# First attention in batches of four cells: one cell per row group, six score banks in three rotating pairs

## The reference, cut to what matters

```python
q = _l2norm(proj(Wq)); k = _l2norm(proj(Wk)); v = proj(Wv)
attn = jnp.einsum('bhqd,bhkd->bhqk', q, k)
rel = pos[None, :] - pos[:, None]
mask = (rel < 0) | (rel >= WINDOW)
bias = jnp.where(mask[None], NEG_INF, -abs(rel) * slopes[:, None, None])
attn = jax.nn.softmax(attn + bias[None], axis=-1)
out = jnp.einsum('bhqk,bhkd->bhqd', attn, v)     # then @ Wo.T, and x = x + out
```

## Time and profile before

| | us |
|---|---|
| median of 3 runs | 460.81 |
| lowest, highest | 457.39, 463.28 |
| profiled execution | 462.66 |
| its span (first to last instruction) | 460.9 |
| PE busy | 380.2 (83%) |
| DVE busy | 261.1 (57%) |
| ACT busy | 163.3 (35%) |
| POOL busy | 141.0 (31%) |

### The profile page before, as it was taken

How to read it: one execution, slowest core, us unless ns; L and a number is a source line. 1 busy time by engine, 2 the same in 40 slices (tenths; PEclk the granted TensorE clock), 3 DMA queues, 4 the chain that set the end, 5 groups by cost and what they waited for, 6 DMA issues and landing times.

```text
span 460.9 us, 12653 instructions
## 1 busy us (share of the span) xinstructions
PE 380.2 (83%) x5430; PEld 285.8 (62%) x5430; DVE 261.1 (57%) x708; ACT 163.3 (35%) x294; POOL 141.0 (31%) x191
## 2 busy tenths in 40 slices
PE   2889999887976706999913679999988998899997
PEld 1677888776856704777711336766765786566665
DVE  7336868876876001444429268776766689633332
ACT  1345547354541303333313222433332304333331
POOL 4012533441428772444425201112112200222221
PEclk9797899999995556999985578999998998899999
DMA  8970200006004112111130000000000000000000
GB/s 239 182 196 1 83 4 4 3 6 253 4 3 146 34 54 72 48 55 47 32 108 0 1 0 4 1 3 3 1 4 4 3 0 2 0 2 23 23 24 23
DMA packets 16199, 19.54 MB, mean 42 GB/s; under 512 B 1376, under 2 KB 14432, under 8 KB 15568
## 3 DMA queue, kind: packets, MB, share of 16 engines
q1 hardware_dynamic: 14896, 16.17, 13.1%
q0 software_dynamic: 1248, 2.57, 1.8%
HBM read 13.60 MB, written 5.13 MB: 41 GB/s over the span
## 4 chain that ended last, share of the span: by engine, by line
PE 64%; DVE 17%; POOL 6%; issue 5%; ACT 3%; DMA 3%; POOLq 0%; SPq 0%; DVEq 0%
PE ps L396 6%; PE ps L1228 4%; PE ps L1310 4%; PE ps L1197 4%; PE ps L374 4%; PE ps L795 3%; POOL xs L1001 3%; PE ps L778 3%; PE ps L779 3%; PE ps L1212 3%; DVE RP L517 3%; PE ps L1237 3%; PE ps L1289 3%; PE ps L1294 2%; PE ps L317 2%
## 5 line engine op out<-in xcount | busy, mean ns | idle before, releaser
L517 DVE TENSOR_TENSOR RP<-ps,RC 128x1440 f32<-128x1440 f32 (+2 forms) x30 | 46.5, 1573 | 8.0 <-PE ps L374 7.9
L659 ACT ACTIVATE RP<-RP 128x1440 f32<-128x1440 f32 (+2 forms) x30 | 40.2, 1340 | 30.1 <-DVE RP L517 30.1
L1562 POOL TENSOR_TENSOR RA<-RA,sm 128x512 f32<-128x512 f32 x18 | 18.8, 1047 | 89.5 <-DVE sm L1404 89.5
L1568 POOL TENSOR_TENSOR RP<-RP 128x512 f32<-128x512 f32 x16 | 16.7, 1042 | 73.4 <-DVE RP L1435 73.4
L396 PE MATMUL ps<-RP,RA 128*32 128x160 f32 (+4 forms) x736 | 33.1, 259 | 4.4 <-DVE LGS L542 3.1
L396 PE MATMUL ps<-RP,con 128*32 128x160 f32 (+4 forms) x736 | 33.0, 256 | 2.7 <-issue 2.7
L691 POOL TENSOR_SCALAR RA<-sm,con 128x512 f32<-128x512 f32 x13 | 20.4, 1587 | 43.4 <-DVE sm L462 43.4
L1009 POOL DMA_INDIRECT ys<-RP x23 | 22.0, 958 | 37.1 <-ACT RP L973 28.1
L374 PE MATMUL ps<-RC,RA 32*128 32x160 f32 x512 | 31.2, 320 | 0.9 <-DVE RA L470 0.6
L884 DVE TENSOR_TENSOR RP<-RP,ps 128x352 f32<-128x352 f32 x23 | 12.0, 521 | 30.5 <-ACT RP L967 30.5
L374 PEld LDWEIGHTS ps<-RC,RA 32*128 32x128 f32 x512 | 25.3, 191 | 5.1 <-issue 2.9
(11 more groups left out here) (245 smaller groups left out, 864.9 us busy)
## 6 DMA issues: line engine op xcount, KB each, us to landing
RA<-in_gu SPq DMA_DIRECT2D x1, 2816.0 KB, 10.2
RB<-in_dw SPq DMA_DIRECT2D x1, 1536.0 KB, 21.2
xs<-zero SPq DMA_DIRECT2D x1, 1483.5 KB, 15.9
RP<-xs SPq DMA_DIRECT2D x5, 258.0 KB, 2.7
RC<-in_tz SPq DMA_DIRECT2D x1, 1120.0 KB, 5.6
X<-in_x SPq DMA_DIRECT2D x4, 256.0 KB, 5.0
XN<-ys SPq DMA_DIRECT2D x4, 256.0 KB, 3.6
out<-X SPq DMA_DIRECT2D x3, 256.0 KB, 2.3
```

Of the source, the lines that this page charges most:

```text
L517: e.tensor_tensor(out.rearrange("p k (i c) -> p k i c", i=n), bank.rearrange("p k (i c) -> p k i c", i=n), bias.unsqueeze(2).to_broadcast( ...
L659: e.activation(v, v, ACT.Exp).then_inc(S["exp"], 1)
L1562: e.tensor_tensor(heads32(m.AT[c % 4]), heads32(m.D1[c % 4]), over(m.R1_[c % 4], 32), ALU.mult).then_inc(S["at1"], 1)
```

## The change

Scores are made per batch: 12 products (24 records), strip by strip, each strip on the four row groups into four banks. Banks 0 to 5 are three *pairs*. A user takes a pair: the first and second half of a batch's scores (`h` = 0, 1: groups 0, 1 and 2, 3), the two halves of a serve, and an output (one pair). A user waits for the one three pairs back. PE's `scores(b)` waits for both of its pairs before its first product.

- VectorE adds the bias in two halves of 128 x 960, ScalarE takes exp in two halves. `P` is a ring of three batches.
- `pv(s)` is now called per strip, for batch b - 2 after the scores of batch b, and counts strips. Only the accumulations use banks 6 and 7; outputs go to a pair of the rotating banks, so the wait of `pv` for `finished` goes away.
- Output k is issued after the value products of batch `ends_in(k) + 2`, that is in loop `ends_in(k) + 4`: in loops 7, 10, 13, 15, 18, 21, 23, 23. Eviction and division of block k stand in loop `ends_in(k) + 2`: 5, 8, 11, 13, 16, 19, 21; ScalarE evicts between its two exps.
- The division's multiplication of blocks 0 to 6 moves from VectorE to GpSimd (`divided`), between the parts of `wide`, `keys` and `norm`. Block 7's stays on VectorE.
- Serves come after the scores of batches 0, 5 and 9. All four value copies of a serve are ScalarE's. A serve's first half is free again when `normal` has read it, its second when ScalarE has copied it.
- X gets rows of 136 words, 128 of X and 8 of logits, so `finished` is one addition of 272 elements.
- SyncE loads `gu` after 15 batches.

The diff, cut:

```diff
+SERVED = {0: 1, 5: 2, 9: 3}
+def last_strip(k):
+    return min(8 * k + 11, NSTRIP - 1)
+def ends_in(k):
+    return last_strip(k) // 3
+def outputs_after(b):
+    return [k for k in range(8) if min(ends_in(k) + 2, NB - 1) == b]
+def order_of_turns():
+    turns = []
+    for b in range(NB + 2):
+        if b < NB:
+            turns.append(("scores", b))
+        if b in SERVED:
+            turns.append(("serve", SERVED[b]))
+        if b >= 2:
+            turns += [("output", k) for k in outputs_after(b - 2)]
+    return turns
+TURNS = order_of_turns()
+PAIRS = [(kind, k, h) for kind, k in TURNS for h in range(1 if kind == "output" else 2)]
+def pair_of(kind, k, h=0):
+    return 2 * (PAIRS.index((kind, k, h)) % 3)
+def wait_pair(w, kind, k, h=0):
+    n = PAIRS.index((kind, k, h)) - 3
     if n >= 0:
-        kind, k = TURNS[n]
-        if kind == "set":
-            w.wait_ge("ad", k + 1)
+        kind, k, h = PAIRS[n]
+        if kind == "scores":
+            w.wait_ge("ad", 2 * k + h + 1)
+        elif kind == "output":
+            w.wait_ge("x1", k + 1)
+        elif h == 0:
+            w.wait_ge("qn", 2 * k + 2)
         else:
-            w.wait_ge("qn", 2 * k + 2)
-            w.wait_ge("vba", 2 * k + 2)
-            w.wait_ge("vbv", 2 * k + 2)
+            values_made(w, k)
...
     def serve(b):
-        wait_turn(w, "serve", b)
+        wait_pair(w, "serve", b, 0)
         expand(b)
+        wait_pair(w, "serve", b, 1)
         values(b)
...
+    def scores(b):
...
+        for h in range(2):
+            wait_pair(w, "scores", b, h)
+        for i in range(len(strips_of(b))):
...
+            for g in range(4):
+                r = slice(32 * g, 32 * g + 32)
+                t = e.matmul(PS[pair_of("scores", b, g // 2) + g % 2][:, 160 * i:160 * i + 160], m.KB[r, s, :, :],
+                             m.QT[r, 32 * s:32 * s + 160], start=True, stop=True)
         t.then_inc(S["sc"], 1)
...
+    def pv(s):
+        q, end = max(0, 32 * (s - 4)), 32 * (s + 1)
+        w.wait_ge("exp", 2 * (s // 3) + 2)
...
-                if k >= 3:
-                    w.wait_ge("x1", 2 * (k - 2))
...
+    for b in range(NB + 2):
+        if b < NB:
+            scores(b)
+        if b in SERVED:
+            serve(SERVED[b])
+        if b >= 2:
+            for s in strips_of(b - 2):
+                pv(s)
+            for k in outputs_after(b - 2):
                 output(k)
...
+    def biased(b, h):
+        n = len(strips_of(b))
+        w.wait_ge("sc", b + 1)
...
         w.wait_ge("dn", 3 * k + 2)
+        if k:
+            w.wait_ge("otn", k)
         e.transpose(m.RT, m.RS.rearrange("p (j h) -> p j h", h=4).unsqueeze(3).to_broadcast([128, 8, 4, 8])
                     ).then_inc(S["dn"], 1)
-        w.wait_ge("dn", 3 * k + 3)
-        if k >= 2:
-            w.wait_ge("mwo", k - 1)
-        e.tensor_tensor(m.OTN[k % 2], ev[:, 0:256], m.RT, ALU.mult).then_inc(S["otn"], 1)
+        if k == 7:
+            divided(e, w, S, m, 7)
...
+    for kind, b in TURNS:
+        if kind == "scores":
+            biased(b, 0)
+            biased(b, 1)
+            for k in range(7):
+                if ends_in(k) + 2 == b:
                     normed(k)
+        elif kind == "serve":
+            normal(b)
+        else:
+            if b == 7:
+                normed(7)
+            finished(b)
+            stats(b)
+def divided(e, w, S, m, k):
+    w.wait_ge("dn", 3 * k + 3)
+    if k >= 2:
+        w.wait_ge("mwo", k - 1)
+    e.tensor_tensor(m.OTN[k % 2], m.EV[k % 2][:, 0:256], m.RT, ALU.mult).then_inc(S["otn"], 1)
...
+    for kind, b in TURNS:
+        if kind == "scores":
+            weights(b, 0)
+            for k in range(7):
+                if ends_in(k) + 2 == b:
                     out(k)
+            weights(b, 1)
+        elif kind == "serve":
+            values(b, range(4))
     out(7)
...
+    wide(0)
+    keys(0)
+    wide(1)
+    keys(1)
+    wide(2)
+    divided(e, w, S, m, 0)
+    keys(2)
+    wide(3)
+    divided(e, w, S, m, 1)
+    keys(3)
+    divided(e, w, S, m, 2)
+    divided(e, w, S, m, 3)
+    norm(0)
+    divided(e, w, S, m, 4)
+    norm(1)
+    divided(e, w, S, m, 5)
+    divided(e, w, S, m, 6)
+    norm(2)
+    norm(3)
...
-    w.wait_ge("sc", 20)
+    w.wait_ge("sc", 15)
     e.dma_start(m.RA[:, 0:5632], t["gu"]).then_inc(S["ldgu"], 16)
```

More of the change, by code:

```diff
@@ L117, in __init__ @@
         self.trif = RC[:, 3136:3392]
-        self.P = RP[:, 0:5760]
+        self.P = [RP[:, 1920 * k:1920 * k + 1920] for k in range(3)]
         self.QK = [RD[:, 1024 * k:1024 * k + 1024] for k in range(4)]
@@ L256, in finish_banks @@
-    return m.PS[k:k + 3]
+    if b == 0:
+        return m.PS[5:8]
+    k, v = pair_of("serve", b, 0), pair_of("serve", b, 1)
+    return [m.PS[k], m.PS[k + 1], m.PS[v]]
 def keys_made(w, b):
@@ new lines, in pv @@
+    def pv(s):
+        q, end = max(0, 32 * (s - 4)), 32 * (s + 1)
+        w.wait_ge("exp", 2 * (s // 3) + 2)
+        values_made(w, s // 16)
+        while q < end:
+            k = q // 256
+            stop = min(end, 256 * (k + 1))
+            first = s == 8 * k
+            if k >= 2:
+                w.wait_ge("evo", k - 1)
+            for half in range(2):
+                for g in range(4):
+                    at = 256 * half + q % 256
+                    t = e.matmul(sum_bank(m, k)[32 * g:32 * g + 32, at:at + stop - q],
+                                 m.ones4 if half else m.VB[:, s, g, :],
+                                 m.cell(s // 3, g, 160 * (s % 3) + q - 32 * (s - 4), stop - q),
+                                 start=first and half == 0, stop=True, skip_group_check=True)
+            q = stop
@@ L495, in attention0_vector @@
                         ALU.mult).then_inc(S["kbv"], 1)
-    values(0)
+    values()
     roots(2)
@@ L551, in stats @@
             e.bn_aggr(m.mv[:, 2 * c:2 * c + 2], m.st[:, 6 * c:6 * c + 6]).then_inc(S["bn1"], 1)
[L553 to L557, removed]
-        for b in range(NB - 1):
-            if ahead(b) == u:
-                for k in range(8):
-                    if output_before(k) == b:
-                        finished(k)
-                        stats(k)
-                for k in ended(b):
-                    normed(k)
-    normed(7)
-    for k in (6, 7):
-        finished(k)
-        stats(k)
+    for kind, b in TURNS:
[4 more added lines that the diff above has]
+                if ends_in(k) + 2 == b:
+                    normed(k)
+        elif kind == "serve":
[7 more added lines that the diff above has]
+    w.wait_ge("dn", 3 * k + 3)
+    if k >= 2:
+        w.wait_ge("mwo", k - 1)
+    e.tensor_tensor(m.OTN[k % 2], m.EV[k % 2][:, 0:256], m.RT, ALU.mult).then_inc(S["otn"], 1)
 def newton_step(e, w, S, m, a, b, k, name, base, after, value):
@@ L617, in values @@
         w.wait_ge("zvb", 2)
-        for h in range(2, 4):
+        for h in heads:
             r = slice(32 * h, 32 * h + 32)
@@ L646, in attention0_scalar @@
     roots(2)
-    values(0)
+    values(0, (2, 3))
     projected(3, 0)
@@ L695, in attention0_gpsimd @@
     e.memset(m.RA[:, 10240:16384], 0.0).then_inc(S["zvb"], 1)
-    for b in range(4):
-        wide(b)
-        keys(b)
     def norm(g):
@@ L720, in norm @@
                             ALU.subtract, ALU.mult).then_inc(S["xn1"], 1)
-    for g in range(4):
-        norm(g)
+    wide(0)
[17 more added lines that the diff above has]
+    norm(3)
 GROUPS = (NTS + 3) // 4
```

174 lines of the change are left out of this document (52 added, 122 removed).

## The result

The changed kernel's median is 455.12 us (20 executions, 450.4 to 462.9), that of the kernel before 464.59 (20, 457.4 to 473.7). The ratio is 0.9845, 95% interval 0.9804 to 0.9886: 1.1 to 2.0% faster, inside the 2% that was called no change. The forecast was 456.7, range 451 to 463, "within 2%" with 0.82. The time fell in the range and on the expected side, but the gain was larger than the 4.1 us of the forecast: 7.2 us by the ratio. The profiled execution took 455.35 us (span 453.5) against 462.66 (span 460.9).

The account below looks back on a forecast made before the run. PE was taken to set the pace, VectorE close behind. Stage 57.0 + 4.1 + 3.45 + 2.5 = 67.0 us against 72.1, 5.1 gained, plus 0.7 tail, less 1.7 clock: 460.8 becomes 456.7 us, range 451 to 463.

Parts of the forecast that it names:

- The fourth joins the same pass: Scores on PE: a fourth row group shares the passes of three, so a batch of 24 records costs 1.02 us.
- The slow rival: Scores on PE: the fourth row group doesn't share passes, 1.84 us a batch, 468 us in all; chance 0.07.
- Stand at batch 5: PE stands 3.45 us before scores(6), because `normal(2)` comes behind `normed(0)` on VectorE.
- The other gates: Scores wait for VectorE's first add, late where `normed` runs: 0.6 to 1.1 us each, 4.1 us in sum.
- The load: PE stands with nothing to wait for after the expert weights' load starts: 2.3 + 0.2 us.
- PE's work: PE's busy time in the stage of the first attention's scores and value products: 57.0 us after the change.
- The clock: The stand at batch 5 pulls PE's clock to half, costing 1.7 us, bounds 0 and 3.4.
- the clock stays up: Rival: PE's clock doesn't fall at batch 5, 455.0 us; chance 0.18.
- The tail: Between the end of batch 19's products and `norm(2)`, VectorE loses a multiplication and a short add: 0.7 us gained.
- The net: Whole kernel: 5.8 us gained from stage and tail, less 1.7 for the clock, 4.1 us.
- The base: Whole kernel: the median of three runs before the change, 460.8 us, from which 456.7 was forecast.
- The rival in which VectorE eats the gain: VectorE is the bound, each batch 0.35 us later, 6 us more in all: about 461 to 462 us; chance 0.20.

Follow-up runs that it names:

- groups_in_turn: Changed kernel with the second serve after batch 4, a batch's 12 products ordered group by group instead of strip by strip; 470.58 us in a single execution.
- normal_first: Changed kernel with `normal(2)` ahead of `normed(0)` on VectorE in batch 5, nothing else changed; 452.73 us, ratio 0.9671 to the kernel before.
- gu_late: Changed kernel with the second serve after batch 4, and `gu` loaded after 22 batches of scores instead of 15; ratio 0.9816 to the kernel before.
- normed_between: `gu_late` with VectorE's `normed` (block 6 excepted) one batch later, between the two bias adds; 452.24 us, ratio 0.9709 to the kernel before.
- a_again: The changed kernel profiled and timed again with nothing edited; ratio 0.9735 to the kernel before.
- weights_late: Changed kernel with the second serve after batch 4, five other weight loads moved from the start into the loop; 450.28 us, ratio 0.9714 to the kernel before.

## Why the prediction was right, and where it was off

- **Scores.** "The fourth joins the same pass": predicted 1.02, measured 1.03 us per batch. `groups_in_turn` shows the mechanism: with most of the sharing gone the batch costs 2.15. The slow rival, 1.84 a batch, is ruled out by the 1.03 itself. (Its sum reads 17 x 0.82 = 13.5; that is 13.9, so its time is 468.6.) The Trainium skill, TensorEngine Tiling (Array Packing), Key Properties, says that a change of tiling mode drains the array. `groups_in_turn` doesn't change how often that happens, so by this rule alone it would cost nothing; the 1.12 us a batch come from the sharing of passes. No run here measures the drain by itself; it is at most part of the 0.2 us that a batch's scores take beyond their six passes.
- **VectorE.** Adds of 1.16 and 2.22 predicted, 1.15 and 2.22 measured. **ScalarE** 1.0, measured 1.00. **GpSimd** 0.6 in bounds of 0.2 to 1.04, measured 0.73, hidden, as said.
- **Stand at batch 5.** 3.45 predicted, 3.31 measured, released by `normal` as foretold. `normal_first` removes it.
- **The other gates.** 4.1 predicted after 8, 11, 13, 16 and 19; measured 0.51 + 0.81 + 0.79 + 0 + 0.67 = 2.78. After batch 13 the stand came out at 0.79 instead of 1.1 (0.91 and 1.06 in the other two executions). That of batch 16 is missing, because PE had just stood 1.35 us without a releaser; in `gu_late`, where it hadn't, it is there with 0.71. I added stalls as if they could not overlap. I also took the first add as the gate everywhere; behind an output it is both adds, which cost nothing here and sets the pace in `normed_between`.
- **The load.** 2.5 predicted; 2.05 measured, in two pieces of 0.70 and 1.35. Only the second is the load's; the first lies before it. The kernel before has 3.2 us of this kind, and likewise 0.9 of it lie before its load.
- **PE's work.** This is a step that failed without being seen. The sum gave 57.0 + 1.7 for the clock = 58.7 us; the windows show 60.22. I had found 1.9 us of work beyond the sum in the kernel before, called them restarts, and left them out for the one after. The 1.5 us too few cancel the 1.8 us by which the stands were too long (8.3 for 10.05), and that 68.7 met 68.49 is luck.
- **The clock.** Half clock with 1.7 us, bounds 0 and 3.4: the three executions gave 1.8, 3.0 and 0. The rival "the clock stays up" is no rival, but the same kernel on another execution. In the profiled pair the 1.8 us don't show, since the kernel before had 6.8 us of half clock in its loop and the one after 3.2 before its stand. That difference is worth 1.8 us in the second row of the table, which shows 1.09: at full clock the changed kernel's start is some 0.8 us longer in each of three executions (14.8 to 15.0 us against 14.1), where the forecast had it equal.
- **The tail.** 0.7 predicted, 0.69 measured.
- **The net.** 5.8 us at full clock were predicted and 5.7 measured, as a mean of three pairs. Of the 7.3 us between the two profiled executions, 2.8 are the chance of the start, 5.3 the loop and -0.8 the rest.
- **The base.** The forecast of 456.7 came out so near 455.12 because two errors met: the median of three, 460.8, was 3.8 us too low (464.59 in 20), and the gain was too small by about 5 against those medians. The ratio times that median gives 7.2 us of gain: 5.7 in the loop, and 1.5 that aren't settled. The nearness of 456.7 is luck.

The rival in which VectorE eats the gain didn't come about for a plain batch, but `normed_between` shows that VectorE is next: once the other stands are gone, what is left waits for L530, and there for the second add behind an output.

## What to carry to other kernels

Products with few rows share passes fully only when neighbours in the queue lie on different row groups: fill all groups, one after the other, before you come back to the first. When the leading engine's work is cut, list who gates it in each loop and in what order the gating engine does its items; the largest single loss here was one item too far back in a queue (3.3 of 8.3 us), cured by moving one call. When PE is idle and nothing released it, look at the packets of its instruction queue, and at which loads run beside them. A single profiled pair can be 3 us apart ahead of the first changed instruction, and one program's executions 8; cut the time at marks before you explain a difference.

## What the runs showed of the hardware

- **The same stand, three answers of the clock.** After 3.3 us with PE idle, TensorE's clock fell to 1.2 GHz for 3.4 us, for 6.8 us, or stayed at 2.4 GHz, in three executions of one program. Shorter stands vary in the same way: after 1.96 us in `a_again` and 1.98 in `weights_late` the clock fell within 0.5 us (119.24, 111.39), after 2.01 in `normal_first` and 2.33 in the kernel before it stayed up. Half clock ahead of scores(0) varied as much: 16.2 to 23.1 and again from 40.1 in one execution of the changed kernel, 16.8 to 23.7 and 33.9 to 54.4 in another.
- **The clock and the time.** Over all timed executions (33 of the kernel before, 26 of the changed one) the mean granted clock was 0.882 before and 0.888 after; within each kernel 0.01 of it goes with some 3 us. By that slope 2 us of the raw difference of the means (465.6 and 456.5 us) go with the clock and some 7 remain. Whether the higher clock is a result of the change or chance stays open.
- **PE stands without a semaphore.** 0 to 2.7 us near 31.5, while the loads of the start run, 1.35 to 2.4 us beside the load of 2816 KB, and shorter ones elsewhere. All 31 of 0.45 us or more end 1.2 to 1.5 us after a 16 KB packet of the instruction queue has landed, and in the changed kernel and its variants they lie at only five places of PE's program. Beside the load the packet starts 7.2 to 9.5 us after the one before, without it 3.7 to 5.5.
